# Last stage of a two-block kernel: two of its norms applied by ScalarE, and a new order around them

## The reference, cut to what matters

```python
src = src + _moe_attn(src, ...)                  # summed by the stage before, kept in SBUF ("acc")
src = _ln(src, ln1_g, ln1_b)                     # first norm, gain g1, bias h1
src2 = jax.nn.relu(src @ W1 + b1) @ W2 + b2      # 256 -> 1024 -> 256
ffn = _ln(src + src2, ln2_g, ln2_b)              # second norm, gain g2, bias h2
x = x + _layernorm(ffn, axis=-1)                 # third norm, no gain; output
```

## Time and profile before

| what | value |
| --- | --- |
| median of three runs | 4069.31 us (4068.82 to 4069.96) |
| the profiled execution, its own time | 4069.74 us |
| its span in the profile | 4067.9 us |
| busy share of the span: PE, DVE, ACT, POOL | 91%, 81%, 48%, 67% |
| the last stage in the span | from 3788 us to the end |
| there, 280 us: PE, DVE, ACT, POOL busy | 210.84, 229.01, 111.48, 132.38 us |

### The profile page before, as it was taken

The page is one execution under the profiler, slowest core; times in us unless marked ns, Lnnn a source line. Parts: engine busy times, 40 slices in busy tenths (PEclk is TensorE's granted clock), DMA queues, the critical chain, the costliest instruction groups (busy, mean ns, idle before and its releaser), DMA issues. The chain is left out here.

```text
span 4067.9 us, 55014 instructions
## 1 busy us (share of the span) xinstructions
PE 3706.3 (91%) x16000; PEld 2539.0 (62%) x16000; DVE 3307.9 (81%) x3879; ACT 1962.4 (48%) x3646; POOL 2717.1 (67%) x2844
## 2 busy tenths in 40 slices
PE   6888988888649999999999999999999999999786
PEld 2344434443337777777777777777777777777675
DVE  5999999999928787878787878778788778787698
ACT  4645664566324444454445454545454445444443
POOL 3767776777636677667667667667667667766354
PEclk9999999999969999999999999999999999999898
DMA  2101110111030001001001001001000000000111
GB/s 75 52 37 37 63 68 37 37 62 63 21 134 16 10 16 39 15 15 39 13 18 37 12 10 44 15 10 44 10 15 17 37 10 21 11 15 10 33 41 36
DMA packets 53667, 131.92 MB, mean 32 GB/s; under 512 B 4223, under 2 KB 33791, under 8 KB 47073
## 3 DMA queue, kind: packets, MB, share of 16 engines
q1 hardware_dynamic: 52560, 127.02, 8.7%
q0 software_dynamic: 1040, 4.19, 0.3%
HBM read 114.16 MB, written 17.04 MB: 32 GB/s over the span
## 5 line engine op out<-in xcount | busy, mean ns | idle before, releaser
L371 POOL TENSOR_TENSOR state<-state,c_rows 128x1024 f32<-128x1024 f32 x256 | 604.1, 2363 | 266.8 <-DVE state L790 265.5
L1320 ACT ACTIVATE prob<-ps_b,negmax 128x512 f32<-128x512 f32 x512 | 345.8, 686 | 653.1 <-DVE negmax L1439 653.1
L790 DVE TENSOR_TENSOR_SCAN state<-dA,ps_a 128x1024 f32<-128x1024 f32 x256 | 584.6, 2284 | 29.9 <-PE ps_a L503 7.9
L503 PE MATMUL ps_a<-state,ident 128*128 128x512 f32 x1024 | 504.7, 617 | 70.9 <-DVE yz L802 70.5
L666 ACT ACTIVATE dA<-dt,a_neg 128x511 f32<-128x511 f32 x512 | 338.7, 712 | 452.3 <-DVE state L790 451.9
L1433 DVE TENSOR_TENSOR vg<-ps_b,gates 128x1024 f32<-128x1024 f32 x256 | 313.4, 1224 | 251.7 <-PE ps_b L1158 239.7
L1047 POOL TENSOR_TENSOR qk_full<-vg 128x512 f32<-128x512 f32 x256 | 329.4, 1287 | 254.2 <-DVE vg L1433 254.2
L1060 POOL TENSOR_TENSOR ogT_low<-prob,ogT_high 128x512 fp32r<-128x512 f32 x256 | 324.3, 1302 | 207.5 <-ACT ogT_high L1353 207.5
L1156 PE MATMUL ps_b<-ogT_high,wo_high 128*128 128x512 f32 x1024 | 412.9, 403 | 11.1 <-DVE ogT_low L1485 10.8
L1156 PE MATMUL ps_b<-wv_high,xT_high 128*128 128x512 f32 x1024 | 414.0, 404 | 0.0
L1158 PE MATMUL ps_b<-ogT_high,wo_low 128*128 128x512 f32 x1024 | 404.2, 395 | 0.0
(11 more groups left out here) (233 smaller groups left out, 8571.3 us busy)
## 6 DMA issues: line engine op xcount, KB each, us to landing
xT<-xT_scratch SPq DMA_DIRECT2D x65, 512.0 KB, 3.3
c_rows<-c_scratch SPq DMA_DIRECT2D x32, 1024.0 KB, 5.5
wv<-in_wv SPq DMA_DIRECT2D x8, 1024.0 KB, 4.9
wo<-in_wo SPq DMA_DIRECT2D x8, 1024.0 KB, 7.0
x_in<-in_x SPq DMA_DIRECT2D x8, 512.0 KB, 4.8
x_a<-in_x SPq DMA_DIRECT2D x8, 512.0 KB, 7.2
x_scratch<-x_a SPq DMA_DIRECT2D x8, 512.0 KB, 2.8
xT_scratch<-x2T SPq DMA_DIRECT2D x8, 512.0 KB, 2.7
```

What stands on the lines that cost most here:

```text
L371: pool.tensor_tensor(state, state, c_rows[:, n, :].unsqueeze(1).to_broadcast([P, HALF, S]), ALU.mult).then_inc(hc_done, 1)
L503: mm = pe.matmul(ps[:, Y_BANK + m, :], ident[:, :], h[s % RING][:, m, :], start=(n == 0), stop=(n == NS - 1))
L790: dve.tensor_tensor_scan(h[s % RING][:, :, :].rearrange("p c s -> p (c s)"), dA[s % RING][:, :, :].rearrange("p c s -> p (c s)"), ps[:, DB ...
L1320: act.activation(prob[h][:, t, :], ps[:, score_bank(t) + h, :], ACT.Exp, bias=negmax[:, t, h:h + 1], accum_out=total[:, h, t:t + 1]).then_ ...
```

## The change

Five things are done at once in `stage_c`; the stages before it are the same.

1. A sixth small operation in `newton` makes `shift` = -mean * rstd, and ScalarE applies the second and the third norm as rstd * x + shift (`apply`: four activations of 128x256, with a per-partition scale and bias). The first norm stays on VectorE and gets the sixth operation too.
2. On VectorE, the whole first norm of the next sequence stands ahead of the second norm's Newton step, and `aT_low` ahead of the third norm's statistics.
3. On ScalarE, the second norm is applied behind the eighth pair and ahead of `keep_a`, and the third norm at the very end of the turn, ahead of the next turn's `take`.
4. On TensorE, the transposes of the next `a` stand behind the first quarter of the outputs.
5. `h` has eight places, and the hidden blocks use six PSUM banks (2 to 7) instead of four.

```diff
--- before.py
+++ after.py
@@ -57,6 +57,7 @@
         self.stats = buf("stats", TT * 6)
         self.avg, self.var, self.apart, self.spread = (buf(w, TT) for w in ("avg", "var", "apart", "spread"))
         self.logv, self.guess, self.step, self.rstd = (buf(w, TT) for w in ("log", "guess", "step", "rstd"))
+        self.shift = buf("shift", TT)
 
     COMBINE = 6
 
@@ -93,7 +94,7 @@
 
     def newton(self, dve, i):
 
-        done, at = self.newton_done, i * 5
+        done, at = self.newton_done, i * 6
         dve.wait_ge(self.guess_done, i * 2 + 2)
         dve.tensor_scalar(self.step[:, :], self.variances(), 1.0 / D, EPS, ALU.mult, ALU.add).then_inc(done, 1)
         dve.wait_ge(done, at + 1)
@@ -106,6 +107,7 @@
         dve.tensor_tensor(self.rstd[:, :], self.guess[:, :], self.step[:, :], ALU.mult).then_inc(done, 1)
         dve.wait_ge(self.combine_done, i * self.COMBINE + self.COMBINE)
         dve.wait_ge(done, at + 5)
+        dve.scalar_tensor_tensor(self.shift[:, :], self.avg[:, :], -1.0, self.rstd[:, :], ALU.mult, ALU.mult).then_inc(done, 1)
 
     def gather(self, dve, rows):
 
@@ -157,6 +159,12 @@
     def ready(self, dve, i):
 
         dve.wait_ge(self.newton_done, i * 5 + 5)
+
+    def apply(self, act, i, rows, out):
+
+        act.wait_ge(self.newton_done, i * 6 + 6)
+        for t in range(TT):
+            act.activation(out(t), rows(t), ACT.Identity, bias=self.shift[:, t:t + 1], scale=self.rstd[:, t:t + 1]).then_inc(self.out_done, 1)
 
     def normalise(self, dve, rows, out):
 
@@ -1587,7 +1595,7 @@
         ab = sb("ab", [P, TT, D])
         w1_parts, w2_parts = parts("w1", [P, KD, F]), parts("w2", [P, FB, D])
         aT = parts("aT", [P, KD, S])
-        h = sb("h", [P, 2, S])
+        h = sb("h", [P, FB, S])
         hT = parts("hT", [P, FB, S])
         f, fn, on = (sb(n, [P, TT, D]) for n in ("f", "fn", "on"))
         x1 = sb("x1_c", [P, TT, D])
@@ -1611,7 +1619,7 @@
             return v[:, :].unsqueeze(1).to_broadcast([P, TT, D])
 
         def h_bank(m):
-            return 4 + (m + 2) % 4
+            return (6, 7, 2, 3, 4, 5, 6, 7)[m]
 
         def turns(eng, turn):
 
@@ -1639,7 +1647,7 @@
         def _(pool):
             def low_hidden(i, m):
                 pool.wait_ge(h_high, i * FB + m + 1)
-                pool.tensor_tensor(hT[1][:, m, :], h[:, m % 2, :], hT[0][:, m, :].bitcast(F32), ALU.subtract).then_inc(h_low, 1)
+                pool.tensor_tensor(hT[1][:, m, :], h[:, m, :], hT[0][:, m, :].bitcast(F32), ALU.subtract).then_inc(h_low, 1)
 
             def add_bias(i, has_back):
                 pool.wait_ge(a_done, i + 1)
@@ -1689,6 +1697,7 @@
                 pe.wait_ge(a_done, b + 1)
                 if not first:
                     pe.wait_ge(aT_low, b)
+                    pe.wait_ge(h_done, (b - 1) * FB + 4)
                 for k in range(KD):
                     for t in range(TT):
                         mm = pe.transpose(ps[:, 2 + k, t * P:(t + 1) * P], a[:, t, k * P:(k + 1) * P], ident[:, :])
@@ -1697,10 +1706,12 @@
             def hidden(i, m, has_back):
                 if m == 0:
                     pe.wait_ge(aT_low, i + 1)
-                if m == 2 and has_back:
+                    if has_back:
+                        pe.wait_ge(h_done, i * FB)
+                elif m == 4 and has_back:
                     pe.wait_ge(f_done, i)
-                if m >= 4:
-                    pe.wait_ge(h_done, i * FB + m - 3)
+                elif m >= 6:
+                    pe.wait_ge(h_done, i * FB + m - 5)
                 for k in range(KD):
                     mm = product(ps[:, h_bank(m), :], lambda u: w1_parts[u][:, k, m * P:(m + 1) * P], lambda u: aT[u][:, k, :], k == 0, k == KD - 1)
                 mm.then_inc(h_psum, 1)
@@ -1710,9 +1721,9 @@
                     if t == 0:
                         pe.wait_ge(h_low, i * FB + m + 1)
                         if m == 0:
-                            pe.wait_ge(h_done, i * FB + FB - 1)
+                            pe.wait_ge(h_done, i * FB + 5)
                     if t == 2 and m == 0:
-                        pe.wait_ge(h_done, i * FB + FB)
+                        pe.wait_ge(h_done, i * FB + 6)
                     mm = product(half(4, t), lambda u: hT[u][:, m, t * P:(t + 1) * P], lambda u: w2_parts[u][:, m, :], m == 0, m == FB - 1)
                 if t == TT - 1:
                     mm.then_inc(f_psum, 1)
@@ -1725,10 +1736,10 @@
                 for m in range(2, FB):
                     hidden(i, m, has_back)
                 outputs(i, 0)
+                if has_front:
+                    turn_a(i + 1)
                 outputs(i, 1)
                 outputs(i, 2)
-                if has_front:
-                    turn_a(i + 1)
                 outputs(i, 3)
 
             turn_acc(0, first=True)
@@ -1748,35 +1759,45 @@
                 act.wait_ge(aT_psum, b + 1)
                 act.activation(aT[0][:, :, :], ps[:, 2:4, :], ACT.Copy).then_inc(aT_high, 1)
 
-            def relu(i, m):
+            def relu(i, m, has_back):
                 act.wait_ge(h_psum, i * FB + m + 1)
-                if m >= 2:
-                    act.wait_ge(h_low, i * FB + m - 1)
-                act.activation(h[:, m % 2, :], ps[:, h_bank(m), :], ACT.Relu, bias=b1[:, m:m + 1]).then_inc(h_done, 1)
+                if m == 0 and has_back:
+                    act.wait_ge(h_low, i * FB)
+                act.activation(h[:, m, :], ps[:, h_bank(m), :], ACT.Relu, bias=b1[:, m:m + 1]).then_inc(h_done, 1)
 
             def high_hidden(i, m):
                 act.wait_ge(h_done, i * FB + m + 1)
-                act.activation(hT[0][:, m, :], h[:, m % 2, :], ACT.Copy).then_inc(h_high, 1)
-
-            def hidden(i, blocks):
+                act.activation(hT[0][:, m, :], h[:, m, :], ACT.Copy).then_inc(h_high, 1)
+
+            def hidden(i, blocks, has_back):
                 for m in blocks:
-                    relu(i, m)
+                    relu(i, m, has_back)
                     high_hidden(i, m)
+
+            def norm2(c):
+                ln2.apply(act, c, lambda t: f[:, t, :], lambda t: fn[:, t, :])
+
+            def norm3(c):
+                act.wait_ge(y_done, CREDIT + c)
+                ln3.apply(act, c, lambda t: o[:, t, :], lambda t: on[:, t, :])
 
             def turn(i, has_back, has_front):
                 if has_front:
                     take(i + 1)
-                hidden(i, (0, 1))
+                hidden(i, (0, 1), has_back)
                 if has_back:
                     ln2.first_guess(act, i - 1)
-                hidden(i, (2, 3))
+                hidden(i, (2, 3), has_back)
                 if has_front:
                     ln1.first_guess(act, i + 1)
-                hidden(i, range(4, FB))
+                hidden(i, range(4, FB), has_back)
+                if has_back:
+                    norm2(i - 1)
+                if has_front:
+                    keep_a(i + 1)
                 if has_back:
                     ln3.first_guess(act, i - 1)
-                if has_front:
-                    keep_a(i + 1)
+                    norm3(i - 1)
 
             act.wait_ge(fill, 1)
             act.preload_act_table_set("natural_log_exp_and_others")
@@ -1789,13 +1810,14 @@
             act.wait_ge(vectors_loaded, all_vectors)
             turns(act, turn)
             ln2.first_guess(act, NB - 1)
+            norm2(NB - 1)
             ln3.first_guess(act, NB - 1)
+            norm3(NB - 1)
 
         @block.vector
         def _(dve):
             rows_s, rows_an = (lambda t: half(0, t)), (lambda t: an[:, t, :])
-            rows_f, rows_fn = (lambda t: f[:, t, :]), (lambda t: fn[:, t, :])
-            rows_o, rows_on = (lambda t: o[:, t, :]), (lambda t: on[:, t, :])
+            rows_f, rows_o = (lambda t: f[:, t, :]), (lambda t: o[:, t, :])
 
             def stats1(b):
                 dve.wait_ge(acc_psum, b + 1)
@@ -1824,10 +1846,8 @@
                 dve.wait_ge(f_done, c + 1)
                 ln2.statistics(dve, c, rows_f)
 
-            def norm2(c):
-
-                ln2.newton(dve, c)
-                ln2.normalise(dve, rows_f, rows_fn)
+            def affine2(c):
+
                 dve.wait_ge(ln2.out_done, c * TT + TT)
                 dve.tensor_tensor(fn[:, :, :], fn[:, :, :], rows(g2), ALU.mult).then_inc(aff2_done, 1)
                 dve.wait_ge(aff2_done, c + 1)
@@ -1836,11 +1856,6 @@
             def stats3(c):
                 dve.wait_ge(o_done, c + 1)
                 ln3.statistics(dve, c, rows_o)
-
-            def norm3(c):
-                ln3.newton(dve, c)
-                dve.wait_ge(y_done, CREDIT + c)
-                ln3.normalise(dve, rows_o, rows_on)
 
             def turn(i, has_back, has_front):
                 b, c = i + 1, i - 1
@@ -1848,15 +1863,15 @@
                     stats2(c)
                 if has_front:
                     stats1(b)
-                if has_back:
-                    norm2(c)
-                if has_front:
```

(12 more changed lines are left out.)

## The result

| kernel | median, us | runs | ratio to before, 95% interval |
| --- | --- | --- | --- |
| before, same chip | 4068.82 (4066.64 to 4071.98) | 7 | |
| changed | 4081.07 (4077.26 to 4085.03) | 7 | 1.0031, 1.0020 to 1.0042 |

The changed kernel is slower by 12.2 us; the forecast was +11.2 on the profiled execution and 4080.5 as a time. The profiled execution of the changed kernel took 4077.26 us, its span is 4075.4. It is one execution of a kernel whose runs spread over 8 us, so I compare lengths inside the last stage: from the start of the first `aT_low` to the end of the last `y` it takes 260.09 us before and 270.70 now, +10.6.

What follows compares the result with a forecast made beforehand. VectorE was taken to set the last stage's pace, its order against GpSimd's run deciding. Loop +8.9, turn 0 +2.4, turn 7 -2.0, tail +1.9 sum to +11.2 us: 4080.9 profiled, 4080.5 predicted, range 4064 to 4090.

Steps and rivals of the forecast that it cites:

- loop: Last stage, six intervals between the `f` additions of turns 1 and 7: 192.2 us against 183.29, +8.9.
- turn 0: Last stage's first turn: TensorE idles before the transposes of `a`, `f` starts at 3838.0, not 3835.56: +2.4 us.
- turn 7: Turn without a front, up to the last `f`: 27.2 us against 29.20, -2.0.
- tail: End of the stage: two norms at 0.7 more, two `shift` at 0.2, four handovers of 0.04: +1.9 us.
- Steps 1 to 5: Turn's start: third norm on ScalarE, GpSimd's `y` and `ab`, held second statistics, guesses, held first Newton; ends at 17.2 us.
- step 8: Turn's end on VectorE: `aT_low`, third statistics, guess, Newton and `shift` end at 32.5 us; turn about 32.4.
- TensorE's path: In the loop: transposes of `a` and three quarters of outputs end at 31.4 us, hidden by VectorE's 32.4.
- the last rival: Chance 0.10: all six first-norm Newton operations held, 4095 us; near it a lower clock, 2.9 over a quarter of outputs.
- Step 3: Second statistics on VectorE, held by `y`, `ab`, first `hT_low`: variance at 8.5 us, cost +2.0; 0 if short operations slipped through.
- No change: Rival, chance 0.25: ScalarE's second column operand is free and `shift` is not held: 4070 to 4073 us.
- faster: Rival, chance 0.13: GpSimd's run does not meet the first norm's Newton steps; turn 28.4 us, time 4054.
- Slower still: Rival, chance 0.10: all six first Newton and `shift` operations held, 7.6 us: +2.4 in six turns, 4095.

Runs made afterwards that it cites:

- no_shift1: The changed kernel without the first norm's sixth small operation (`shift`): 4075.37 us, 1.0016 of before.
- turn_a_late: The changed kernel with the transposes of `a` back in front of the last quarter of outputs: 4077.31 us, 1.0018 of before.
- order_only: The changed kernel with second and third norm applied by VectorE again and no `shift`: 4072.81 us, 1.0009 of before.
- order_only_mid: As order_only, with the transposes of `a` behind the second quarter of outputs instead of the first: 4069.02 us, 0.9998 of before.
- mid_noshift1: The changed kernel with the transposes of `a` behind the second quarter and no `shift` for the first norm: 4071.13 us, 1.0005 of before.
- the best version: The changed kernel with `y` behind the next turn's eighth `hT_low` and second Newton, transposes behind the second quarter, no first-norm `shift`: 4063.85 us, 0.9990 of before.

## Why the prediction was right

Point by point, in us from the end of the third norm's `shift` (3929.14 + 0.16 in the rows above; the next ends at 3961.38), forecast against measured:

| step | forecast | measured |
| --- | --- | --- |
| 1 four activations with two column operands | 2.07 (0.585 each) | 2.08 (0.588 to 0.602) |
| 2 `y` starts, `ab` ends | 2.35, 7.1 | 2.42, 7.17 |
| 3 second variance | 8.5 | 8.52 |
| 4 first Newton starts | 12.05 | 12.03 |
| 5 first Newton and `shift` | 5.2 | 5.07 |
| 6 `a` is there | 21.7 | 21.43 |
| 7 gain of `fn` starts; bias ends | 25.05; 27.55 | 24.64; 27.13 |
| 8 end of the third `shift` | 32.5 | 32.08 |
| loop | +8.9 | +7.7 |
| turn 0; turn 7; tail | +2.4; -2.0; +1.9 | +2.8; -1.75; +1.84 |

- *Steps 1 to 5.* The mechanism came as forecast, step by step. The rule that spoke against the change held: the Trainium skill, "SBUF — State Buffer", section "SBUF: two separate sides", says that an operation with two SBUF inputs needs the shared ports, and `shift` was held for 1.20 where GpSimd ran and took 0.16 where it did not. no_shift1 gives 0.75 a turn back. The same skill, "ScalarE: Activation LUTs", section "What ACT_TABLE_LOAD costs", prices the second column operand like the first; the trace agrees, with 583 to 602 ns in the loop.
- *Turn 0* is the step of TensorE's idle time, and turn_a_late (2.6 back) and order_only against order_only_mid (1.8) show that it is the position of the transposes.
- *What failed* is in the paragraph behind step 8: that TensorE's path "is hidden by VectorE's 32.4, with 1.0 to spare". The term is the 9.7 us (1.09 + 8.6) from `a` to the next `f`: it measured 11.1 to 12.3, and `f` waited for TensorE at the end of all six turns, 0.4 to 1.6. In the turn shown the transposes took 1.97 instead of 1.09, at the lower clock, and over the loop TensorE spends more time there: (1 - 0.90) x 2 x 191 = 38 us against (1 - 0.97) x 2 x 183 = 11. I had put that only into the last rival. It cost nothing in the loop (turn_a_late), by a reason that I had not seen; that the sum held in spite of it was luck.
- *The attribution was partly wrong, though the sum was right.* Step 3 gave the third norm on ScalarE a cost of 2.0, against a variance at 6.5 behind `f`, which is every second turn only (5.4 in the others). Most of the later variance comes from the order (order_only_mid: 7.67 behind `f`'s start), and the third norm's move by itself gains. And of the 5.6 us a turn that the prediction sees removed from VectorE, 2.9 are removed by the order; what ScalarE then takes over is an unheld 1.38, for a wait of 2.15. The parts from before to the changed kernel, by the stage: order and places +0.8, third norm -3.0, second norm +5.6. The transposes' place and the first `shift` account for the remaining 7.2 (turn_a_late gives 3.8 of it; the rest, 3.4, lies between turn_a_late and mid_noshift1, which differ in the `shift` and by one quarter in the transposes). Sum +10.6. Each part is a difference of two single traces and can be off by some us, by turn 7 alone; the signs of the two norms' parts agree with the times.
- *The rivals.* No change needed a free second operand, and `on` took 2.08, not 1.73. It and faster both needed short operations to slip past GpSimd; of the six behind the first guess four were held (0.96, 1.23, 1.19, 1.20), as assumed. Slower still needed all six. The reason given for the two that passed was partly misread: L101 (3942.32) and L103 behind it ran while GpSimd stood idle for 0.36 us between two `hT_low`, waiting for ScalarE, and so did the prediction's L102 before the change (3968.74, between an `hT_low` that ended at 3968.68 and one that began at 3969.10); only its L78 was issued as GpSimd went from one operation to the next. And the 3.6 us at which the faster rival was to decide do not come out of the prediction's own numbers, which give about 3: 6 less a sixth of 4080.5 - 4061.2 is 2.8, or 3.2 with turn 0's 2.4 taken off first. Nothing rested on it.

## What to carry to other kernels

Price a moved operation by what it costs in the new order, not by its row in the old one: `fn` took 4.23 only because it stood in GpSimd's run, and once the order had freed it, ScalarE's 2.15 for it was a loss. Where two engines block each other, look for the stretch in which the one idles and put the other's long operation there; that was worth 8 us of the stage here in two pairs of traces, more than any other part. A small operation is free only if nothing holds it: drop results that nobody reads. And read more than one turn of a loop: the kernel before had two kinds, and in the best version the one odd turn shows what the clock costs.
